# A two-way scan layer on one core: squares of the gated outputs move to GpSimd, their sums to transposes and VectorE, and all orders are new

## Chip, cores and metric

One core of a Trainium2 chip runs the whole kernel in one launch. The metric is device time in microseconds (us) from a run of the program; the profiled execution was recorded by the hardware profiler. Engines in the profile: PE is TensorE's matmul and PEld its weight load, DVE is VectorE, ACT is ScalarE, POOL is GpSimd, SP is SyncE.

## What is computed

Input x has 8 batches of 512 tokens with 256 channels. Each batch is normalised, goes through a selective-scan block in both token orders, is added back, normalised again, and goes through a linear layer with a low-rank correction.

```
zxbcdt = x @ Win                         # 256 -> 512 z, 512 x, 64 B, 64 C, 8 dt
xBC = silu(conv(xBC, convw, 4 taps) + convb)
dt = softplus(dt + dtb); dA = exp(dt * -exp(Alog))
h = dA_t * h + dt_t * outer(x_t, B_t)    # 8 heads of 64 x 64, token by token
y = C_t . h;  y = y + D * x
y = y * silu(z)
y = y * rsqrt(mean(y * y, over 512) + 1e-5) * normw
out = concat(y_fwd @ Wout_f, flip(y_rev @ Wout_b)) @ Wo + bo
```

All arithmetic is fp32; the projections run as three passes over split high and low parts.

## The kernel before, in words

Channels lie on the 128 partitions and tokens along the row, four chunks of 128. A scan works chunk by chunk in matrix form. `project` (L485 to L487) fills a PSUM bank with 128 channels of one direction, nine tiles in all: tile 0 holds B and C, tiles 1 to 4 the inputs x, tiles 5 to 8 the gates z. `conv_start` (ScalarE, L934) and three `conv` steps (VectorE, L1406) are the convolution, `conv_end` (L943) its Silu, and the ScalarE `gate` (L948) the Silu of z. `dt_project`, `dt_transposed` (L515) and the `soft_` steps give dt; `sums` and `s_transposed` (L530) give the running decays, which `row_copy` (L920) and `row_decays` (L925) write out so that SyncE can spread them over all partitions (`put_rows`, `repeat_heads`, `put_decays`, `repeat_decays`). `bound` (L964) and `decay` (L970) turn them into factors, `weights` (VectorE, L1433) multiplies them by the scores. `b_tokens` (TensorE L536, ScalarE L989) and `x_tokens` (L545, VectorE L1418) transpose B and x to have tokens on partitions. `state` (L565) makes the chunk states from xw (`decayed_x` on GpSimd, L1906, which needs `w_end` from `decay_w`, L952). `intra` (L578) and `inter` (L590) add up the outputs of a pair of heads; `inter` p needs `decayed_c` p (GpSimd, L1912). `outputs` (VectorE, L1455) adds D times x, and GpSimd's `gate` (L1929) multiplies by silu(z), giving yg.

The mean square of yg over its 512 channels: ScalarE squares the four tiles (`square`, L984; the first into sqsum, the others in turn into two buffers sq), GpSimd adds them to sqsum (`add_square`, L1937), and TensorE's `squares` (L598) multiplies each 128 x 128 chunk of sqsum by a column of ones, so that each token's sum stands in column c of the bank, and VectorE copies the four columns to ss (L1468). GpSimd's `mean_square` and `rms_root` follow. Beside that `mix` (L612) projects yg, and VectorE's `mix` (L1476) scales it with rms and adds it to the residual xres. `norm2_`, `feed` and `store` finish the batch. The reversed scan of the last batch has its own ending (`last_square`, `last_sums`, ...), with squares on ScalarE.

The work is laid out by hand: each engine has its own list of steps for the opening, the first scan, the reversed scan, the forward scan and the last scan. A loop turn runs the reversed scan of batch b, beside which the forward projections of batch b + 1 run, and then the forward scan of batch b + 1, with the reversed projections of b + 1 and the second norm and feed of batch b. There are seven such turns. Between engines there are only semaphores, and each engine runs its list strictly in order. The small PSUM results share two banks, taken in turn in the order of the lists START, LOOP and LAST, so a result waits until the one before the last is drained. VectorE and GpSimd also run `s_neg` (L1388), `s_rest` (wd, L1394) and `keep_x` (L1847).

Three wait rules hold the parts of the squares together:

```
act.wait_ge(yg_ready, KI * u + t + 1)            # square: its tile of yg
act.wait_ge(sqsum_ready, u)                      # square 1: the use before is summed
pool.wait_ge(sq_step, KI * u + t + 1)            # add_square: its square
```

## Time and profile before

| | |
|---|---|
| median of 3 runs | 636.88 us (635.69 to 637.5) |
| profiled execution, its own time | 635.01 us |
| its span, first to last instruction | 633.2 us |
| mean granted TensorE clock | 0.997 of full speed |
| instructions | 13301 |

How to read it: busy time is the time in which an engine has an instruction in hand; the span is cut into stretches where that helps. The chain is followed back from the last instruction, at each step to what released it. A group is all instructions of one line and shape. TensorE's matmuls are pipelined: the record of each is longer than its distance to the next, which is what the chain's pieces show.

### The profile page before, as it was taken

The numbers are of one execution on the slowest core, as the hardware profiler recorded it, in microseconds if no ns is written. First come the engines' busy times: TensorE is split into PE (matmuls) and PEld (weight loads), VectorE is DVE, ScalarE is ACT, GpSimd is POOL, SyncE is SP. The second block draws the span as 40 slices with busy tenths as digits, with TensorE's granted clock in tenths as the row PEclk, the third lists the DMA queues.
The fourth block names the chain that finished last, engine by engine and source line by source line (L and its number), as shares of the span: only waits on it lengthen the run. The fifth ranks groups of instructions, "written<-read, shape, count | busy, mean of one in ns | idle before, by whom it ended". The sixth has DMA issues, their size and how long they took to land.

```text
span 633.2 us, 13301 instructions
## 1 busy us (share of the span) xinstructions
PE 602.9 (95%) x3996; PEld 492.4 (78%) x3996; DVE 510.0 (81%) x1056; ACT 545.8 (86%) x1220; POOL 363.1 (57%) x367
## 2 busy tenths in 40 slices
PE   2998999999999999999999999999999999999995
PEld 1676788887888878887888878888788878888784
DVE  3779788986979689797888869798797978788663
ACT  4799998979997998979989799889989799897862
POOL 1026656666575664765556675656647665465933
PEclk9999999999999999999999999999999999999998
DMA  7552614245160632407132361505416071332600
GB/s 223 158 180 92 208 23 132 57 119 192 25 184 0 193 116 65 144 9 248 51 126 83 98 211 25 182 3 177 131 29 180 1 217 59 101 111 67 211 1 33
DMA packets 43544, 70.70 MB, mean 112 GB/s; under 512 B 8000, under 2 KB 30592, under 8 KB 43520
## 3 DMA queue, kind: packets, MB, share of 16 engines
q1 hardware_dynamic: 43520, 70.40, 36.5%
q8 instruction: 12, 0.20, 0.1%
q14 instruction: 12, 0.10, 0.1%
HBM read 59.37 MB, written 4.72 MB: 101 GB/s over the span
## 4 chain that ended last, share of the span: by engine, by line
PE 80%; ACT 9%; DVE 5%; issue 3%; POOL 2%; DMA 0%; SPq 0%; POOLq 0%; ACTq 0%; DVEq 0%
PE mi L612 17%; PE pj L485 9%; PE py L578 9%; PE pj L487 9%; PE pj L486 9%; PE py L590 6%; PE mi L565 4%; PE mi L678 3%; PE mi L545 2%; PE mi L598 2%; ACT bs L964 2%; ACT L952 1%; DVE xdt L1418 1%; POOL xw L1906 1%; PE mi L671 1%
## 5 line engine op out<-in xcount | busy, mean ns | idle before, releaser
L1406 DVE SCALAR_TENSOR_TENSOR xc<-pj,cw,xc 128x509 f32<-128x509 f32 (+2 forms) x240 | 173.9, 742 | 20.5 <-ACT xc L934 19.1
L964 ACT ACTIVATE bs<-bs,s_all 128x128 f32<-128x128 f32 x512 | 159.3, 392 | 0.0
L1929 POOL TENSOR_TENSOR yg<-yg,sz 128x512 f32<-128x512 f32 x60 | 76.6, 1287 | 87.3 <-DVE yg L1455 87.3
L485 PE MATMUL pj<-xnt_hi,w_hi 128*128 128x512 f32 x288 | 121.2, 421 | 3.8 <-DVE xnt_lo L1323 2.9
L487 PE MATMUL pj<-xnt_hi,w_lo 128*128 128x512 f32 x288 | 114.1, 396 | 0.0
L486 PE MATMUL pj<-xnt_lo,w_hi 128*128 128x512 f32 x288 | 113.9, 395 | 0.0
L612 PE MATMUL mi<-wc,yg 128*128 128x256 f32 x480 | 110.9, 384 | 0.0
L612 PEld LDWEIGHTS mi<-wc,yg 128*128 128x128 f32 x480 | 88.7, 190 | 14.0 <-issue 3.2
L1937 POOL TENSOR_TENSOR sqsum<-sqsum,sq 128x512 f32<-128x512 f32 x45 | 57.9, 1287 | 60.7 <-ACT sq L984 60.0
L1433 DVE TENSOR_TENSOR bs<-bs,gm 128x512 f32<-128x512 f32 x128 | 85.9, 676 | 6.7 <-ACT bs L970 6.3
L1906 POOL TENSOR_TENSOR xw<-xdt,w_end 128x512 f32<-128x512 f32 x48 | 49.7, 1044 | 48.7 <-DVE xdt L1418 37.5
L970 ACT ACTIVATE bs<-bs 128x512 f32<-128x512 f32 x128 | 77.1, 622 | 0.2
L1418 DVE TENSOR_TENSOR xdt<-mi,dt 128x512 f32<-128x512 f32 x64 | 43.2, 687 | 36.2 <-PE mi L545 35.9
L485 PEld LDWEIGHTS pj<-xnt_hi,w_hi 128*128 128x128 f32 x288 | 54.7, 190 | 18.3 <-DVE w_lo L1293 3.3
L578 PE MATMUL py<-bs,xdt 128*64 128x128 f32 x1024 | 67.4, 277 | 1.6 <-DVE yg L1455 1.6
L934 ACT ACTIVATE xc<-pj,cb,cw 128x512 f32<-128x512 f32 x80 | 61.3, 766 | 8.3 <-PE pj L487 7.8
L578 PEld LDWEIGHTS py<-bs,xdt 128*64 128x64 f32 x1024 | 56.1, 137 | 13.7 <-issue 6.6
L487 PEld LDWEIGHTS pj<-xnt_hi,w_lo 128*128 128x128 f32 x288 | 54.4, 189 | 12.7
L1912 POOL TENSOR_TENSOR es<-cc,es 128x384 f32<-128x384 f32 x64 | 63.7, 1007 | 0.6
L486 PEld LDWEIGHTS pj<-xnt_lo,w_hi 128*128 128x128 f32 x288 | 54.8, 190 | 9.9
L590 PE MATMUL py<-es,hst 128*128 128x128 f32 x384 | 55.5, 281 | 0.2 <-DVE hst L1447 0.2
L590 PEld LDWEIGHTS py<-es,hst 128*128 128x128 f32 x384 | 49.3, 192 | 4.3 <-issue 2.9
(151 smaller groups left out, 1040.3 us busy)
## 6 DMA issues: line engine op xcount, KB each, us to landing
bs<-rows_dram SPq DMA_DIRECT2D x64, 512.0 KB, 5.0
es<-rows_dram SPq DMA_DIRECT2D x128, 96.0 KB, 3.3
cc<-bcm SPq DMA_DIRECT2D x32, 128.0 KB, 3.1
xres<-in_x SPq DMA_DIRECT2D x8, 512.0 KB, 3.8
out<-ot SPq DMA_DIRECT2D x32, 128.0 KB, 3.7
xin<-in_x SPq DMA_DIRECT2D x7, 512.0 KB, 4.1
cz<-bcm SPq DMA_DIRECT2D x16, 128.0 KB, 3.4
rows_dram<-s_rows SPq DMA_DIRECT2D x128, 4.0 KB
```

Source lines behind the costliest of these rows:

```text
L485: pe.matmul(ps[:], hi(k), xnt_hi[:, k, :], start=(k == 0), stop=False)
L486: pe.matmul(ps[:], hi(k), xnt_lo[:, k, :], start=False, stop=False)
L487: mm = pe.matmul(ps[:], lo(k), xnt_hi[:, k, :], start=False, stop=(k == KD - 1))
L578: pe.matmul(py[bank][HP * half:HP * half + HP, Q * c:Q * c + Q], xdt[:, c, HP * h:HP * h + HP], bs[:, h, Q * c:Q * c + Q], start=(c == 0), ...
L590: mm = pe.matmul(py[bank][:, Q * c:Q * c + Q], hst[:, j, p, :], es[:, p, Q * c:Q * c + Q], start=False, stop=(j == NC - 2), skip_group_che ...
L612: mm = pe.matmul(ps[:, D * i:D * i + D], yg[:, d, t, Q * c:Q * c + Q], wc[:, d, t, :], start=(t == 0), stop=(t == KI - 1))
L964: i = nc.scalar.activation(bs[:, h, Q * c:Q * c + Q], bs[:, h, Q * c:Q * c + Q], ACT.Relu, bias=s_all[:, d, 0, c, h:h + 1], scale=-1.0)
L970: nc.scalar.activation(bs[:, h, :], bs[:, h, :], ACT.Exp, scale=-1.0).then_inc(decayed, 1)
L1406: i = dve.scalar_tensor_tensor(xc[:, t, to], pj[bank][:, of], cw[:, d, t, KW - 1 - s:KW - s], xc[:, t, to], ALU.mult, ALU.add)
L1433: dve.tensor_tensor(bs[:, h, :], bs[:, h, :], gm[:], ALU.mult).then_inc(m_ready, 1)
L1912: pool.tensor_tensor(es[:, p, LATER[d]], cc[:, d, LATER[d]], es[:, p, LATER[d]], ALU.mult).then_inc(c2_ready, 1)
L1929: pool.tensor_tensor(yg[:, d, p, :], yg[:, d, p, :], sz[:, d, p, :], ALU.mult).then_inc(yg_ready, 1)
```

## The change

The squares of yg are taken by GpSimd (a product of the tile with itself) instead of ScalarE. TensorE's `squares` transposes the four chunks of sqsum into a PSUM bank instead of multiplying them by ones, and VectorE's `squares` sums the bank over its 128 columns per chunk instead of copying four columns. `b_tokens` transposes only B's 64 lanes, into 64 columns per chunk, with a semaphore instruction ahead of it, and ScalarE copies the 256 columns that now lie side by side. All lists of steps of all engines, and with them the lists of PSUM banks, are in a new order. `last_square` stays on ScalarE. The diff below is cut: of the opening, the first and the last scan nothing is shown, of VectorE's lists only two places. Indentation is reduced.

In the parts left out: in the opening, `dt_project` goes before the first `project`; ScalarE has `split_high` 0 and 1 and `split_dt_high`, VectorE the matching `split_low` and `split_dt_low`, ahead of the first `norm_high` and `norm_low`; the constants are loaded after the first weights. In the forward scan VectorE keeps s_neg and s_rest at its end, ahead of the last `outputs`.

```diff
--- before.py
+++ after.py
@@ the lists of banks @@
-START = (["a0", "a1", "dtm", "dtt", "w0", "w1", "w2", "w3", "0S", "0ST", "w4", "w5", "w6", "w7", "w8"]
-+ ["0bt", "0x0", "0x1", "0x2", "0s0", "0x3", "1S", "1ST", "0s1", "0s2"])
+START = (["a0", "a1", "dtm", "dtt", "w0", "w1", "w2", "w3", "0S", "w4", "0ST", "w5", "w6", "w7", "w8"]
++ ["0x0", "0bt", "0x1", "1S", "0s0", "1ST", "0x2", "0x3", "0s1", "0s2"])
 LOOP = ["1bt", "1x0", "1x1", "1x2", "1x3", "a0", "a1", "1s0", "1s1", "dtm", "dtt", "0ss", "0o0", "1s2",
-"0o1", "0S", "0ST", "0bt", "0x0", "0x1", "0x2", "0s0", "0x3", "1ss", "0s1", "0s2", "1o0", "1o1",
+"0o1", "0S", "0ST", "0x0", "0bt", "0x1", "0x2", "0x3", "0s0", "1ss", "0s1", "0s2", "1o0", "1o1",
 "1S", "1ST", "t0", "t1", "f0", "f1", "t2", "t3", "f2", "f3"]
-LAST = ["1x0", "1x1", "1x2", "1bt", "1x3", "1s0", "0ss", "1s1", "0o0", "1s2", "0o1", "1o0", "1o1"]
+LAST = ["1x0", "1x1", "1bt", "1x2", "1x3", "1s0", "0ss", "1s1", "0o0", "0o1", "1s2", "1o0", "1o1"]
 assert len(LOOP) % 2 == 0
@@ SyncE @@
 def turn(it, more):
+    copy_c(it + 1, 0)
     if more:
         load_x("loop", it, it + 2)
-    copy_c(it + 1, 0)
     put_rows("loop", it, it + 1, 0)
     repeat_heads(it + 1, 0, 0)
+    repeat_heads(it + 1, 0, 1)
+    repeat_heads(it + 1, 0, 2)
     put_decays(it + 1, 0)
-    repeat_heads(it + 1, 0, 1)
     repeat_decays(it + 1, 0, 0)
-    repeat_heads(it + 1, 0, 2)
     repeat_decays(it + 1, 0, 1)
+    repeat_heads(it + 1, 0, 3)
     repeat_decays(it + 1, 0, 2)
-    repeat_heads(it + 1, 0, 3)
     repeat_decays(it + 1, 0, 3)
+    copy_c(it + 1, 1)
     put_rows("loop", it, it + 1, 1)
     store("loop", it, it, 0)
     load_residual(it + 1)
+    put_decays(it + 1, 1)
     repeat_heads(it + 1, 1, 0)
...
@@ TensorE, b_tokens @@
+    alone(pe)
     for c in range(NC):
-        mm = pe.transpose(ps[:, P * c:P * c + P], bcm[:, d, Q * c:Q * c + Q], ident)
+        mm = pe.transpose(ps[:, NS * c:NS * c + NS], bcm[0:NS, d, Q * c:Q * c + Q], ident[0:NS, 0:NS])
@@ TensorE, squares @@
     for c in range(NC):
-        mm = pe.matmul(ps[:, c:c + 1], sqsum[:, Q * c:Q * c + Q], ones[:, 0:1], start=True, stop=True)
+        mm = pe.transpose(ps[:, Q * c:Q * c + Q], sqsum[:, Q * c:Q * c + Q], ident)
@@ TensorE @@
 def reversed_scan(phase, it, b, nxt):
     more = phase == "loop"
+    project(b, 1, NT - 1)
     b_tokens(phase, it, b, 1)
     x_tokens(phase, it, b, 1, 0)
-    project(b, 1, NT - 1)
     x_tokens(phase, it, b, 1, 1)
     x_tokens(phase, it, b, 1, 2)
     x_tokens(phase, it, b, 1, 3)
     norm_transposed(phase, it, nxt)
     scores(phase, it, b, 1)
     state(phase, it, b, 1, 0)
+    state(phase, it, b, 1, 1)
     wait_xnt(phase, it)
-    state(phase, it, b, 1, 1)
     project(nxt, 0, 0)
     dt_project(phase, it)
     project(nxt, 0, 1)
     project(nxt, 0, 2)
     dt_transposed(phase, it)
+    intra(b, 1, 0)
     squares(phase, it, b, 0)
     mix(phase, it, b, 0, 0)
     mix(phase, it, b, 0, 1)
     state(phase, it, b, 1, 2)
-    intra(b, 1, 0)
     intra(b, 1, 1)
     mix(phase, it, b, 0, 2)
     mix(phase, it, b, 0, 3)
     inter(phase, it, b, 1, 0)
-    sums(phase, it, nxt, 0)
     inter(phase, it, b, 1, 1)
     project(nxt, 0, 3)
-    project(nxt, 0, 4)
+    sums(phase, it, nxt, 0)
     intra(b, 1, 2)
     s_transposed(phase, it, nxt, 0)
     inter(phase, it, b, 1, 2)
+    project(nxt, 0, 4)
     intra(b, 1, 3)
     inter(phase, it, b, 1, 3)
     project(nxt, 0, 5)
@@ TensorE @@
 def forward_scan(phase, it, b, last):
     more = phase == "loop"
     project(b, 0, NT - 1)
+    x_tokens(phase, it, b, 0, 0)
     b_tokens(phase, it, b, 0)
-    x_tokens(phase, it, b, 0, 0)
     scores(phase, it, b, 0)
     x_tokens(phase, it, b, 0, 1)
     x_tokens(phase, it, b, 0, 2)
     project(b, 1, 0)
+    x_tokens(phase, it, b, 0, 3)
     state(phase, it, b, 0, 0)
-    x_tokens(phase, it, b, 0, 3)
     project(b, 1, 1)
     project(b, 1, 2)
     squares(phase, it, last, 1)
...
     mix(phase, it, last, 1, 2)
     mix(phase, it, last, 1, 3)
     sums(phase, it, b, 1)
+    intra(b, 0, 1)
+    inter(phase, it, b, 0, 1)
     project(b, 1, 3)
     project(b, 1, 4)
-    intra(b, 0, 1)
     s_transposed(phase, it, b, 1)
-    inter(phase, it, b, 0, 1)
+    intra(b, 0, 2)
     norm2_transposed(phase, it, last, 0)
-    intra(b, 0, 2)
     inter(phase, it, b, 0, 2)
     norm2_transposed(phase, it, last, 1)
     feed(phase, it, 0)
...
     norm2_transposed(phase, it, last, 2)
     intra(b, 0, 3)
     norm2_transposed(phase, it, last, 3)
-    inter(phase, it, b, 0, 3)
     feed(phase, it, 2)
     feed(phase, it, 3)
+    inter(phase, it, b, 0, 3)
     project(b, 1, 5)
     project(b, 1, 6)
     project(b, 1, 7)
@@ ScalarE @@
 def b_tokens(phase, it, d):
     ps, free = misc(phase, it, f"{d}bt")
-    src = ps[:].rearrange("p (c n) -> p c n", c=NC)[:, :, 0:NS]
-    nc.scalar.activation(btok[:], src, ACT.Copy).then_inc(free, 1)
+    nc.scalar.activation(btok[:], ps[:, 0:NC * NS].rearrange("p (c n) -> p c n", c=NC), ACT.Copy).then_inc(free, 1)
@@ ScalarE @@
 def reversed_scan(phase, it, b, nxt):
     more = phase == "loop"
     b_tokens(phase, it, 1)
-    bound(b, 1, 0)
     gate(b, 1, NT - 1)
     decay_w(b, 1)
+    bound(b, 1, 0)
+    norm_high(phase, it, 0)
     decay_e(b, 1)
-    norm_high(phase, it, 0)
     norm_high(phase, it, 1)
     decay(b, 1, 0)
     bound(b, 1, 1)
     bound(b, 1, 2)
+    conv_start(nxt, 0, 0)
     bound(b, 1, 3)
-    square(phase, it, b, 0, 3)
-    conv_start(nxt, 0, 0)
     decay(b, 1, 1)
     dt_bias(phase, it)
     decay(b, 1, 2)
     conv_start(nxt, 0, 1)
+    bound(b, 1, 4)
     soft_exp(nxt)
-    bound(b, 1, 4)
     decay(b, 1, 3)
+    decay(b, 1, 4)
     bound(b, 1, 5)
-    decay(b, 1, 4)
+    conv_start(nxt, 0, 2)
     decay(b, 1, 5)
     soft_log(nxt)
-    conv_start(nxt, 0, 2)
+    conv_end(nxt, 0, 0)
     bound(b, 1, 6)
-    conv_end(nxt, 0, 0)
+    decay(b, 1, 6)
     bound(b, 1, 7)
-    decay(b, 1, 6)
     decay(b, 1, 7)
+    row_copy(phase, it, 0)
     conv_start(nxt, 0, 3)
-    square(phase, it, b, 1, 0)
+    conv_end(nxt, 0, 1)
     conv_start(nxt, 0, 4)
-    row_copy(phase, it, 0)
-    square(phase, it, b, 1, 1)
     row_decays(phase, it, 0)
-    conv_end(nxt, 0, 1)
     gate(nxt, 0, 5)
     conv_end(nxt, 0, 2)
     conv_end(nxt, 0, 3)
     gate(nxt, 0, 6)
+    gate(nxt, 0, 7)
     conv_end(nxt, 0, 4)
-    square(phase, it, b, 1, 2)
-    square(phase, it, b, 1, 3)
-    gate(nxt, 0, 7)
@@ ScalarE @@
 def forward_scan(phase, it, b):
     more = phase == "loop"
     ahead = not (isinstance(b, int) and b == NB - 1)
+    bound(b, 0, 0)
     b_tokens(phase, it, 0)
     gate(b, 0, NT - 1)
     decay_w(b, 0)
-    bound(b, 0, 0)
-    decay_e(b, 0)
     decay(b, 0, 0)
     bound(b, 0, 1)
     conv_start(b, 1, 0)
     decay(b, 0, 1)
+    bound(b, 0, 2)
     conv_start(b, 1, 1)
-    bound(b, 0, 2)
+    decay_e(b, 0)
     bound(b, 0, 3)
+    conv_start(b, 1, 2)
     decay(b, 0, 2)
+    decay(b, 0, 3)
     bound(b, 0, 4)
-    conv_start(b, 1, 2)
-    decay(b, 0, 3)
+    decay(b, 0, 4)
     bound(b, 0, 5)
-    decay(b, 0, 4)
     bound(b, 0, 6)
+    conv_end(b, 1, 0)
     bound(b, 0, 7)
     decay(b, 0, 5)
     decay(b, 0, 6)
-    square(phase, it, b, 0, 0)
-    decay(b, 0, 7)
     conv_start(b, 1, 3)
     norm2_scale(b - 1, 0)
+    norm2_scale(b - 1, 1)
+    row_copy(phase, it, 1)
+    decay(b, 0, 7)
     norm2(phase, it, 0)
-    row_copy(phase, it, 1)
-    norm2_scale(b - 1, 1)
+    norm2(phase, it, 1)
+    norm2_scale(b - 1, 2)
     row_decays(phase, it, 1)
-    norm2_scale(b - 1, 2)
-    norm2(phase, it, 1)
     norm2_scale(b - 1, 3)
-    conv_end(b, 1, 0)
     norm2(phase, it, 2)
     norm2(phase, it, 3)
     if ahead:
         norm1_scale(b + 1, 0)
         norm1_scale(b + 1, 1)
     conv_start(b, 1, 4)
+    conv_end(b, 1, 1)
+    conv_end(b, 1, 2)
+    gate(b, 1, 5)
     if ahead:
         norm1_scale(b + 1, 2)
-    conv_end(b, 1, 1)
-    conv_end(b, 1, 2)
+    conv_end(b, 1, 3)
+    gate(b, 1, 6)
     if ahead:
         norm1_scale(b + 1, 3)
-    square(phase, it, b, 0, 1)
-    square(phase, it, b, 0, 2)
-    gate(b, 1, 5)
-    conv_end(b, 1, 3)
     conv_end(b, 1, 4)
-    gate(b, 1, 6)
     gate(b, 1, 7)
@@ VectorE @@
 def squares(phase, it, d):
     ps, free = misc(phase, it, f"{d}ss")
-    dve.tensor_copy(ss[:, d, :], ps[:, 0:NC]).then_inc(free, 1)
+    dve.tensor_reduce(ss[:, d, :], ps[:].rearrange("p (c n) -> p c n", c=NC), mybir.AxisListType.X, ALU.add).then_inc(free, 1)
@@ VectorE, reversed_scan @@
     norm_low(phase, it, nxt, 0)
     norm_low(phase, it, nxt, 1)
     state(phase, it, b, 1, 0)
+    state(phase, it, b, 1, 1)
     scores(b, 1)
-    state(phase, it, b, 1, 1)
...
-    outputs(b, 1, 0)
+    s_copy(phase, it, 0)
+    s_neg(phase, it, 0)
+    weights(phase, it, b, 1, 6)
     outputs(b, 1, 1)
-    s_copy(phase, it, 0)
-    mix(phase, it, b, 0, 3)
-    weights(phase, it, b, 1, 6)
+    weights(phase, it, b, 1, 7)
     conv(nxt, 0, 3, 1)
-    weights(phase, it, b, 1, 7)
+    outputs(b, 1, 2)
+    s_rest(phase, it, 0)
@@ GpSimd @@
+def square(phase, it, b, d, t):
+    u = 2 * b + d
+    pool.wait_ge(yg_ready, KI * u + t + 1)
+    if t == 0 and phase == "loop":
+        bank, used = misc_use(phase, it, f"{1 - d}ss")
+        pool.wait_ge(mi_full[bank], used + 1)
+    if t == 1 and phase == "loop":
+        pool.wait_ge(sqsum_ready, u)
+    if t == 3:
+        pool.wait_ge(sq_added, (KI - 2) * u + 1)
+    to = sq[:, (t - 1) % 2, :] if t else sqsum[:]
+    pool.tensor_tensor(to, yg[:, d, t, :], yg[:, d, t, :], ALU.mult).then_inc(sq_step, 1)
@@ GpSimd, reversed_scan @@
     decayed_x(phase, it, b, 1, 0)
     decayed_x(phase, it, b, 1, 1)
     decayed_state(phase, it, b, 1, 1)
+    square(phase, it, b, 0, 3)
     add_square(b, 0, 3)
     decayed_state(phase, it, b, 1, 2)
+    decayed_c(b, 1, 0)
+    decayed_c(b, 1, 1)
     decayed_x(phase, it, b, 1, 2)
     mean_square(phase, it, 0)
-    decayed_c(b, 1, 0)
+    decayed_c(b, 1, 2)
     rms_root(b, 0)
-    decayed_c(b, 1, 1)
-    decayed_c(b, 1, 2)
+    gate(b, 1, 0)
+    square(phase, it, b, 1, 0)
     decayed_c(b, 1, 3)
-    gate(b, 1, 0)
     gate(b, 1, 1)
+    square(phase, it, b, 1, 1)
     add_square(b, 1, 1)
     gate(b, 1, 2)
+    square(phase, it, b, 1, 2)
     gate(b, 1, 3)
     add_square(b, 1, 2)
+    square(phase, it, b, 1, 3)
     add_square(b, 1, 3)
@@ GpSimd, forward_scan @@
     rms_root(last, 1)
     decayed_c(b, 0, 2)
     gate(b, 0, 0)
-    decayed_c(b, 0, 3)
+    square(phase, it, b, 0, 0)
     norm2_neg(last)
     norm2_var(last)
+    if ahead:
+        norm1_neg(b + 1)
+        norm1_var(b + 1)
     norm2_root(last)
     norm2_shift(last)
     result_bias(phase, it, last)
     if ahead:
-        norm1_neg(b + 1)
+        norm1_root(b + 1)
     gate(b, 0, 1)
+    square(phase, it, b, 0, 1)
     if ahead:
-        norm1_var(b + 1)
-        norm1_root(b + 1)
         norm1_shift(b + 1)
+    decayed_c(b, 0, 3)
     gate(b, 0, 2)
     add_square(b, 0, 1)
+    square(phase, it, b, 0, 2)
     keep_x(b)
     add_square(b, 0, 2)
     gate(b, 0, 3)
```

## Rows read from the trace of the kernel before

**Rows 1.** Page, part 1: busy us (share of the span) xinstructions.

```profile
PE 602.9 (95%) x3996; PEld 492.4 (78%) x3996; DVE 510.0 (81%) x1056; ACT 545.8 (86%) x1220; POOL 363.1 (57%) x367
```

**Rows 2.** Page, part 4: the chain that ended last, by engine.

```profile
PE 80%; ACT 9%; DVE 5%; issue 3%; POOL 2%; DMA 0%; SPq 0%; POOLq 0%; ACTq 0%; DVEq 0%
```

**Rows 3.** Busy time by stretch: stretch, us, each engine, granted clock, DMA share, GB/s.

```profile
40.00:107.84 67.84, 64.16 (x448) 51.39 (x447) 58.07 (x119) 64.63 (x147) 40.51 (x39) 1.00 0.40 125
182.24:256.64 74.40, 73.44 (x496) 60.34 (x495) 61.97 (x130) 66.72 (x150) 46.14 (x47) 1.00 0.37 110
256.64:331.30 74.66, 73.61 (x496) 60.31 (x495) 63.96 (x130) 66.74 (x151) 46.15 (x47) 1.00 0.34 110
```

**Rows 4.** The chain in one turn: start us, us, what.

```profile
...
230.45 0.36 PE mi L515 x4
230.81 0.98 PE mi L598 x8
...
255.28 0.45 PE mi L536 x4
...
263.52 0.79 PE mi L598 x8
```

**Rows 5.** Groups of TensorE: line, shapes, count, busy us, mean ns, idle.

```profile
L598 PE MATMUL mi<-cst,sqsum 128*128 128x1 f32 x120 | 15.0, 246 | 0.1
...
L536 PE MATMUL mi<-cst,bcm 128*128 128x128 f32 x64 | 9.6, 272 | 0.0
```

**Rows 6.** Groups of ScalarE, the same columns.

```profile
L943 ACT ACT_TABLE_LOAD x24 | 30.8, 1283 | 0.4
L984 ACT ACTIVATE sq<-yg 128x512 f32<-128x512 f32 x45 | 26.6, 625 | 0.2 <-POOL yg L1929 0.2
```

**Rows 7.** Groups of GpSimd, the same columns.

```profile
L1929 POOL TENSOR_TENSOR yg<-yg,sz 128x512 f32<-128x512 f32 x60 | 76.6, 1287 | 87.3 <-DVE yg L1455 87.3
...
L1937 POOL TENSOR_TENSOR sqsum<-sqsum,sq 128x512 f32<-128x512 f32 x45 | 57.9, 1287 | 60.7 <-ACT sq L984 60.0
L1906 POOL TENSOR_TENSOR xw<-xdt,w_end 128x512 f32<-128x512 f32 x48 | 49.7, 1044 | 48.7 <-DVE xdt L1418 37.5 <-ACT w_end L952 11.2
```

**Rows 8.** Timeline of VectorE: start us, us, instructions in order.

```profile
251.76 1.07 DVE L1313 BATCH_NORM_STATS2 st<-xin 128x6 f32<-128x256 f32 x3
```

**Rows 9.** Timelines of TensorE and of ScalarE in one turn; idle in brackets.

```profile
220.68 0.66 PE L545 MATMUL mi<-cst,xs 128*128 128x128 f32 x4 [0.35 <-DVE xdt L1418]
...
222.12 0.66 PE L469 MATMUL mi<-cst,xin 128*128 128x128 f32 x4 [0.19 <-DVE xdt L1418]
...
224.47 0.65 PE L565 MATMUL mi<-xw,btok 128*64 128x256 f32 x4 [0.22 <-issue]
...
259.50 0.65 PE L565 MATMUL mi<-xw,btok 128*64 128x256 f32 x4 [0.20 <-POOL xw L1906]
...
256.64 1.28 ACT L952 ACT_TABLE_LOAD   x1
```

**Rows 10.** Groups of VectorE, columns as in rows 5.

```profile
L1418 DVE TENSOR_TENSOR xdt<-mi,dt 128x512 f32<-128x512 f32 x64 | 43.2, 687 | 36.2 <-PE mi L545 35.9
...
L1328 DVE TENSOR_REDUCE v<-mi 128x64 f32<-128x128 f32 x8 | 2.3, 291 | 6.0 <-PE mi L515 6.0
...
L1468 DVE COPY ss<-mi 128x4 f32<-128x4 f32 x15 | 2.3, 154 | 2.6 <-PE mi L598 2.6
```

**Rows 11.** Timelines of VectorE and of GpSimd at 291 us.

```profile
290.97 2.44 DVE L1394 TENSOR_TENSOR wd<-s_all 128x32 f32<-128x32 f32 x1
...
290.96 2.40 POOL L1847 TENSOR_TENSOR xres<-xres,bo_sb 128x1024 f32<-128x1024 f32 x1
```

**Rows 12.** Timeline of ScalarE, between row_copy and w_end.

```profile
251.14 0.60 ACT L948 ACTIVATE sz<-pj 128x512 f32<-128x512 f32 x1 [1.03 <-PE pj L487]
```

**Rows 13.** Timeline of GpSimd, and the chain, late in a forward scan.

```profile
280.80 1.27 POOL L1929 TENSOR_TENSOR yg<-yg,sz 128x512 f32<-128x512 f32 x1
...
283.62 1.02 PE py L578 x16
```

More of the change, by code:

```diff
@@ new lines, in first_scan @@
+                s_copy(phase, it, 1)
+                conv(b, 1, 0, 2)
+                conv(b, 1, 0, 3)
+                weights(phase, it, b, 0, 0)
+                s_neg(phase, it, 1)
+                conv(b, 1, 1, 1)
+                state(phase, it, b, 0, 0)
+                s_rest(phase, it, 1)
+                conv(b, 1, 2, 1)
+                conv(b, 1, 1, 2)
+                x_tokens(phase, it, 0, 3)
+                conv(b, 1, 1, 3)
+                x_tokens(phase, it, 0, 2)
+                weights(phase, it, b, 0, 1)
```

422 lines of the change are left out of this document (196 added, 226 removed).

## The prediction

> **What bounds the kernel now.** I read the busy shares first, then the chain, then busy time by stretch, then the timelines where two engines meet. TensorE is busy 95% of the span, ScalarE 86%, VectorE 81%, GpSimd 57% [rows 1]; a busy matmul row may still hold a wait, so the shares alone settle nothing. The chain that ended last puts 80% of the span on TensorE, 9% on ScalarE, 5% on VectorE and 2% on GpSimd [rows 2]. The stretches say why. One turn of the loop (one batch, both scans) takes 74.40 us, with TensorE busy for 73.44; ScalarE works 66.72, VectorE 61.97, GpSimd 46.14 [rows 3]. There are seven turns of this kind, an opening and a first batch before them and a tail behind. The granted clock is 1.00 there (the upper level, 2.4 GHz), so the clock is not in play. Inside a turn, what TensorE does not have to do comes off the time, as long as no other engine takes its place.
>
> **The squares' sums on TensorE.** Each of 15 uses is now 4 matmuls of one column; the trace has 120 instructions, so two passes per matmul [rows 5]. The chain gives a use 0.98 us in the reversed scan and 0.79 in the forward one [rows 4], mean 0.887: nearly all of it loads sqsum as the stationary operand, twice. The change makes them transposes. Transposes of just this shape exist: B's tokens have 64 instructions for 16 uses, so one pass each [rows 5], and four of them take 0.45 us in the chain [rows 4]. So a use falls by 0.44 us, and 15 save **6.6 us**. Ends: nothing, should a short group pay a slow start; at most 0.98 - 0.45 = 0.53 each, 8.0 us.
>
> **B's tokens** (16 uses) stay 4 transposes, but of 64 lanes and with 64 columns of identity. No row has that. The nearest is dt's transpose with 32 lanes and 32 columns, which takes 0.36 us for four [rows 4]; so most of the time does not follow the columns. Ends: 0.45 (no gain) and 0.22 (columns alone count). I take 0.37, next to that row: 0.08 x 16 = **1.3 us**. The semaphore instruction put ahead of them only holds a wait; I cost it at nothing, since matmuls of a projection are still in flight while it passes. ScalarE's copy still reads 256 columns: no change.
>
> **ScalarE.** It loses 60 Squares (45 to sq, in the row, and 15 to sqsum) at 0.625 us, 37.5 us [rows 6]. That looks like relief for the engine at 86%, but the new order gives it back. A table load costs 1283 ns [rows 6], and a turn now has seven (ahead of decay_w twice, soft_log, conv_end 0 and 1 of the reversed scan, its late decays, conv_end 0 of the forward scan). I walked the new lists with the same three families (Exp, Ln, Silu; the rest runs under any). In the forward scan conv_end(b, 1, 0) now stands between bound 6 and decay 5: one more load for it and one for the way back to Exp. In the reversed scan row_decays stands behind conv_end(nxt, 0, 1), and a Silu gate follows: two more. 4 x 1.283 = 5.1 us come to a turn, 8 x 0.625 = 5.0 go. ScalarE's work stays at 66.8 of 74 us. What counts is where the loads stand (rival 1).
>
> **GpSimd** gets the 60 squares. Its product of two such tiles takes 1287 ns; one with the same tile twice is not in the trace. Ends: 1044 (the cheapest row over 512 columns) and 1287 [rows 7]; I take 1287, the same two-input form: 77 us in all, 10.3 in a turn, 46.14 becomes 56.4 of 74. As a sum it is covered: it now waits 87 us for VectorE's outputs and 60 for ScalarE's squares [rows 7], and the latter go. Where the reversed scan ends, it must do gate 3, add 2, square 3 and add 3 (5.2 us) after VectorE's last output, which ends as the norm's statistics begin, at 251.76 [rows 8]: done at 257.0. decayed_x then waits for w_end, behind the table load that starts at 256.64 and takes 1.28 [rows 9]: covered, by about 1 us.
>
> **VectorE.** The copy of 4 sums (154 ns) becomes a sum over 512 columns of PSUM. In the rows 128 columns take 291 ns, so (291 - 154)/124 = 1.1 ns for each column more, 0.154 + 508 x 0.0011 = 0.71 us; a product over 512 columns at 0.687 is the other end [rows 10]. I take 0.70: +0.55 x 15 = 8.2 us, 1.1 in a turn, on an engine with 12 us free. In the reversed scan mix 0 waits for it (and a root on GpSimd), but TensorE mixes for 3.6 us meanwhile: covered.
>
> **A lock between VectorE and GpSimd.** wd (32 columns) takes 2.44 us from 290.97, and ends with GpSimd's keep_x of 2.40 us from 290.96 [rows 11]. That turn lasts 74.66 us against 74.40 [rows 3]: a stall of 2.2 us costs 0.26. More GpSimd work makes more such meetings, in the reversed scan above all, where s_neg now follows s_copy while the gates run. If every turn had one, 7 x 0.26 = 1.8 us, less what is there now. I take +0.5.
> The Trainium skill, "SBUF — State Buffer", Who interferes with whom, states that VectorE and GpSimd share a port pair, that VectorE wants it with two SBUF inputs or in a two-port mode, and that the later one is blocked for the whole instruction. By that rule 60 more GpSimd instructions are 60 more chances to block; the trace agrees (2.44 us for wd), and shows how little of it reaches the end.
>
> **The orders.** TensorE's idle in a turn is 0.96 us, and four rows make it up: 0.35 and 0.19 in the run of x_tokens and norm transposes, 0.22 before state 1, 0.20 before the forward state 0 [rows 9]. The new order puts x_tokens 3 ahead of that state 0 (four transposes of work, while xw comes), and state 1 straight behind state 0 instead of behind the wait for xnt: 0.42 go. The run of x_tokens stays paced by xdt (0.687 us [rows 10] for four transposes) and loses the projection in its midst: its stalls stay. So 0.42 x 7 = **2.9 us**, between nothing and 0.96 x 7 = 6.7. Other moves (intra 1 before two projections, sums later) swap work whose inputs are there. load_x on SyncE's queue goes behind copy_c, which waits for conv_end; it is issued some 17 us later, and still lands before 251.76, when the norm reads it. copy_c of the other direction goes ahead of put_rows, and its input comes earlier too: nothing. In the opening dt_project goes first and two splits stand ahead of it; I take that as even.
>
> **Sum**, against the profiled execution (635.01 us, 1.8 above its span): -6.6 - 1.3 - 2.9 + 0.5 = -10.3, so 624.7. The median of the runs, 636.88, is 1.87 above that execution; so **626.6 us**.
>
> **Rivals.**
> 1. *ScalarE's loads take the pace* (slower). From row_copy to the next scan's w_end the list gains two loads (2.57 us) and bound 0 (1.17) and loses four squares (some 0.52 each between neighbours): +1.6. w_end releases xw and so state 0. For it: the wait before state 0 is put down to xw [rows 9]. Against: ScalarE idles 1.03 us in that stretch for a projection [rows 12], which takes most of it up. From a surplus over 1 us on it decides; with all of TensorE's gain hidden and 0.6 more in each turn it is 636.9 + 7 x 0.6 = 641. Chance 0.11.
> 2. *GpSimd makes es late* (no change). In the forward scan decayed_c 3 now stands behind gate 1 and square 1. Gate 1 starts at 280.80 and takes 1.27 [rows 13]; a root goes ahead of it (1.0), square 1 (1.29), a shift and decayed_c itself (1.0) follow: 285.6. inter 3, moved behind two feeds (1.73), wants it 1.73 - 0.44 after intra 3 ends at 284.64 [rows 13], at 285.9. If the sequence is 1.5 us longer, TensorE stalls 1.2 in a turn: 7 x 1.2 = 8.4, so 635.0 to 635.5. For it: a margin of 0.3. Chance 0.10.
> 3. *The new transposes save TensorE little*, because each short group pays its start: 6.6 becomes nothing, 633.2. Against it: 0.45 for four of them in the chain. Chance 0.12.
> 4. *More stalls go than I count*: the other 0.54 us of idle in a turn too (3.8), and 2 of the 3.7 us by which TensorE misses the stretch from 40 to 107.84 [rows 3]: 621. Chance 0.17.
>
> **Numbers.** My case has 0.50. Faster by over 0.3% (what a measurement of this kernel can tell from no change, 1.9 us) are my case, 3 and 4: 0.79; within it 2: 0.10; slower 1: 0.11. Range: from 619, a little under case 4, to 637, past case 2; case 1 is left out, and little else.
>
> **What would show it.** The sums' transposes at x60, four in 0.45 us; B's in 0.37; turns of about 73 us with TensorE idle for 0.5; no Square but the four at the end; 28 more table loads and ScalarE still near 546 us; GpSimd near 440. I am wrong if turns stay at 74 with TensorE idle before state 0 (rival 1) or inter 3 (rival 2), or if a group of these transposes takes 0.8.

## The result, and the profile after

The changed kernel takes 638.4 us (median; 637.7 to 639.17, 14 runs) against 636.81 for the kernel before on the same chip (635.69 to 637.5, 14 runs): ratio 1.0029, 95% interval 1.0021 to 1.0037. It is slower by 1.6 us by the medians and 1.8 by the ratio, just under the bound of 0.3% for a difference; I had forecast 626.6, in a range up to 637.

Page of the changed kernel: busy time and share of each engine, and the chain that ended last; it answers to [rows 1, 2].

```profile
span 637.0 us, 13185 instructions
PE 606.5 (95%) x3936; PEld 482.2 (76%) x3936; DVE 524.6 (82%) x1056; ACT 552.2 (87%) x1188; POOL 422.7 (66%) x427
PE 75%; ACT 11%; DVE 9%; issue 3%; POOL 1%; DMA 0%; SPq 0%; ACTq 0%; DVEq 0%; POOLq 0%
```

TensorE lost 60 matmuls, as meant, but only its weight loads are less busy (482 us against 492); its matmuls are busy for 606.5 us against 602.9. ScalarE has 60 Squares less and is 6 us busier (28 more table loads, as walked); GpSimd rose from 57% to 66%. The chain has less TensorE in it and more ScalarE and VectorE.

One turn of it by stretch, the columns of [rows 3], and the groups that are new (busy us, mean ns, idle before and its releaser):

```profile
148.05:222.67 74.62, 73.78 (x487) 58.81 (x487) 64.47 (x130) 67.96 (x147) 54.13 (x55) 1.00 0.37 112
L599 PE MATMUL mi<-cst,sqsum 128*128 128x128 f32 x60 | 9.4, 279 | 0.0
L1442 DVE TENSOR_REDUCE ss<-mi 128x4 f32<-128x512 f32 x15 | 10.3, 685 | 4.0 <-PE mi L599 4.0
L1916 POOL TENSOR_TENSOR sq<-yg 128x512 f32<-128x512 f32 x45 | 46.9, 1041 | 1.8
```

A turn still takes 74.6 us, where I had said 73. The prices of single instructions came out near what I took, or below: the sum over columns 0.685 us (taken 0.70), GpSimd's square 1.04 (taken 1.29: with the same tile on both sides it is at the cheap end). Four transposes of sqsum are dearer: 0.49 and 0.53 from their start to the next group's (taken 0.45).

Where the 3.8 us between the two profiled spans lie (single executions; the medians are 1.6 us apart). Turns here run from the first norm transpose of one turn to that of the next. From the start of the loop's first turn to that of the seventh (six turns) the kernel before takes 519.50 - 72.31 = 447.19 us, the changed one 521.22 - 73.41 = 447.81: 74.53 and 74.64 a turn. The stretch before the first turn is 1.1 longer; 0.4 of that is a later change of TensorE's pace, no work of the change (last section). The other 0.7 is there again between x1 and x7 (first turn at 73.27 and 73.17) and x4 and x6 (73.94 and 73.90), which open like the changed kernel; I had taken the opening as even. In the seventh turn both reach the last scan's x tokens after 69.8 us; from there on, 43.9 us are left before (589.35 to 633.2) and 45.9 after (591.05 to 637.0). Part of that may belong to the execution: x7 and x14 below have the same code there and take 43.6 and 45.0. In the changed kernel TensorE idles there ahead of the tokens, for nothing that the profile shows, and behind VectorE:

```profile
592.86 0.43 PE L537 MATMUL mi<-cst,bcm 64*128 64x64 f32 x4 [0.75 <-issue]
598.88 5.42 PE L613 MATMUL mi<-wc,yg 128*128 128x256 f32 x24 [0.29 <-DVE ss L1442]
```

The puzzle is in the turns: by my count TensorE was given 0.9 us less work for the sums in each, and a turn did not get shorter.

### The profile page after: what moved, and what is told of

Read it like the earlier page. It is cut to its first block, busy times and chain, and to the rows that moved or that the text cites. A ratio compares the mean times of both kernels' runs of the same rounds, so it can differ in the third digit from the quotient of the medians.

```text
span 637.0 us, 13185 instructions
## 1 busy us (share of the span) xinstructions
PE 606.5 (95%) x3936; PEld 482.2 (76%) x3936; DVE 524.6 (82%) x1056; ACT 552.2 (87%) x1188; POOL 422.7 (66%) x427
## 4 chain that ended last, share of the span: by engine, by line
PE 75%; ACT 11%; DVE 9%; issue 3%; POOL 1%; DMA 0%; SPq 0%; ACTq 0%; DVEq 0%; POOLq 0%
PE mi L613 16%; PE py L579 8%; PE pj L485 8%; PE pj L487 7%; PE pj L486 7%; PE py L591 5%; PE mi L679 4%; PE mi L566 4%; PE mi L546 4%; DVE xc L1380 2%; ACT xs L944 2%; PE gm L553 2%; ACT sz L949 2%; DVE xdt L1392 2%; ACT xc L935 2%
## 5 line engine op out<-in xcount | busy, mean ns | idle before, releaser
L487 PE MATMUL pj<-xnt_hi,w_lo 128*128 128x512 f32 x288 | 114.0, 396 | 0.0
L579 PE MATMUL py<-bs,xdt 128*64 128x128 f32 x1024 | 69.2, 277 | 1.2 <-DVE bs L1407 0.7
L487 PEld LDWEIGHTS pj<-xnt_hi,w_lo 128*128 128x128 f32 x288 | 54.3, 189 | 12.8
L1894 POOL TENSOR_TENSOR hs<-hst,e_end 128x512 f32<-128x512 f32 x32 | 33.4, 1044 | 36.5 <-ACT e_end L956 19.0
L591 PE MATMUL py<-es,hst 128*128 128x128 f32 x384 | 53.9, 280 | 0.3 <-DVE hst L1421 0.2
```

What stands on the lines that cost most here:

```text
L487: mm = pe.matmul(ps[:], lo(k), xnt_hi[:, k, :], start=False, stop=(k == KD - 1))
L579: pe.matmul(py[bank][HP * half:HP * half + HP, Q * c:Q * c + Q], xdt[:, c, HP * h:HP * h + HP], bs[:, h, Q * c:Q * c + Q], start=(c == 0), ...
L591: mm = pe.matmul(py[bank][:, Q * c:Q * c + Q], hst[:, j, p, :], es[:, p, Q * c:Q * c + Q], start=False, stop=(j == NC - 2), skip_group_che ...
```

## The experiments

Each run has the kernel before beside it on the same chip; ratios are to that. "Turn" is the mean of turns 1 to 6, read as above.

```
run                                     ratio   95% interval      turn us
changed kernel                          1.0029  1.0021 to 1.0037  74.64
x1  sums by transposes only             1.0005  0.9995 to 1.0015  74.55
x2  squares on GpSimd only              1.0068  1.0053 to 1.0084  74.88
x3  all three operations, old orders    1.0109  1.0093 to 1.0126  75.36
x4  new orders, sums by ones            1.0063  1.0048 to 1.0079  74.92
x5  small squares (work left out)       1.0077  1.0063 to 1.0091  75.05
x6  small sum (work left out)           0.9969  0.9958 to 0.9979  74.15
x7  x1, sum covered                     0.9921  0.9908 to 0.9934  73.80
x8  new orders, three moves             1.0151  1.0136 to 1.0166  75.55
x9  x7 and B's tokens                   0.9941  0.9928 to 0.9954  73.91
x10 new orders, cover only              1.0044  1.0031 to 1.0058  74.65
x11 x9 and squares on GpSimd            1.0092  1.0077 to 1.0106  75.20
x12 x9, states together                 0.9944  0.9930 to 0.9958  73.91
x13 x7, GpSimd squares behind xw        1.0219  1.0204 to 1.0233  76.25
x14 x7, states together                 0.9931  0.9917 to 0.9944  73.82
```

### Operations or orders?

My first theory was that the operations pay and the new orders give it back. x1 to x3 put operations alone into the kernel before; x4 takes one out of the changed kernel.

```
x1  mm = pe.transpose(ps[:, Q*c:Q*c+Q], sqsum[...], ident)   # for pe.matmul(.., ones[:, 0:1])
    dve.tensor_reduce(ss[:, d, :], ps[...], X, ALU.add)      # for dve.tensor_copy(ss, ps[:, 0:NC])
x2  square(...) out of the lists of act; into those of pool: 0, 1 behind gates 0, 1; 2, 3 ahead of gate 3 and add 3
x3  x1 + x2 + B's tokens from 64 lanes
x4  changed kernel, L599 and L1442 as in the kernel before
```

> The kernel before with its own orders; only the squares' sums go by four transposes and VectorE's sum over columns. Theory (the operations pay, the new orders give it back): the reversed use keeps its 0.35 us per turn, the forward use loses it to the wait of state 2 for the bank that VectorE's sum holds, so 634.3 us, 2.5 below the kernel before (between 632.5 and 635.5). Rival (the transposes save TensorE nothing that counts, since other engines set the pace): 636.4 to 637.4. Rival (my forecast's own term, no bank wait): 630.8.

> The kernel before with its own orders; only the squares of gated outputs move from ScalarE to GpSimd, each in GpSimd's list behind its gate or ahead of its addition. Theory: ScalarE's 60 squares were covered, GpSimd has the room, some VectorE instructions are held beside GpSimd's: 637 us, within 0.7 of the kernel before. Rival (GpSimd's load and the lock are what the change pays): slower by 2 us or more, 639 and above. Rival (ScalarE sets the pace in places): faster by 2 us or more, 635 and below.

> The kernel before with its own orders and all three changed operations (GpSimd's squares, sums by transposes, B's tokens from 64 lanes). Theory (the operations pay and the new orders give it back): the sum of the first two and about 0.5 for B's tokens, 633.5 us (632 to 635), so 5 below the changed kernel. Rival (operations give nothing, orders neutral): 636.5 to 638.5.

> The changed kernel with its new orders, the squares' sums back to the matmul with the column of ones and the short copy. Theory: it loses the reversed use's gain and gets back the bank wait, so 639.9 us, 1.0 to 2.5 slower than the changed kernel. My forecast's term: 6.6 slower, 645. Rival (transposes save nothing): within 0.5 of the changed kernel's 638.4.

The theory fell. x1 gains nothing, x2 costs 0.7% and x3 1.1%: in the old orders the operations themselves lose 7 us, and the new orders win 5 of them back (x3 against the changed kernel). Only x4 came as expected: in the new orders the transposes give 0.28 us a turn, a third of what I had counted.

The waits of TensorE in x1 (us in total, times, longest) say what took its saving:

```profile
PE mi L523 <- DVE al L1376: 3.4, 8, 1.0
PE mi L565 <- DVE ss L1468: 1.6, 7, 0.4
```

In the kernel before, the first of these is one wait of 1.0, and the second isn't there; the wait for xw is 1.4 in both. What is new comes from VectorE's sum. Forward, it still holds its PSUM bank when state 2, two uses on, wants it. Reversed, it stands in VectorE's list between the steps of the softplus (du, rq, dd ... al), so that al comes 20.5 us into the turn instead of 20.0 and is late for the decays' sums. VectorE and TensorE of x1 there:

```profile
233.86 0.68 DVE L1468 TENSOR_REDUCE ss<-mi 128x4 f32<-128x512 f32 x1
242.84 0.18 DVE L1376 TENSOR_SCALAR al<-adt 128x32 f32<-128x32 f32 x1
243.08 0.41 PE L523 MATMUL mi<-al,cst 128*128 128x32 f32 x2 [0.38 <-DVE al L1376]
```

### Is VectorE's sum the price, and what does GpSimd's load cost in the new orders?

```
x5  pool.tensor_tensor(to[:, 0:32], yg[.., 0:32], yg[.., 0:32], mult)      # changed kernel, from the loop on
x6  dve.tensor_reduce(ss, ps[...][:, :, 0:8], X, ALU.add)                  # changed kernel
x7  x1, forward:  state 1, intra 0, state 2      # for state 1, state 2, intra 0
        reversed: inter 0, inter 1, sums         # for inter 0, sums, inter 1
x8  changed kernel, forward as in x7; project(b, 1, NT-1) between x tokens 0 and 1; row_decays ahead of conv_end 1
```

> The changed kernel; from the loop on, each of GpSimd's squares covers 32 of the 512 columns (the first scan's stay whole), so some 57 squares of 1.04 us shrink to a fraction and the output leaves out most of the squares. Turns of the changed kernel are 74.6 us. Theory A (in the new orders GpSimd's squares are off the path, ScalarE's xs and w_end pace the reversed end): turn 74.4 to 74.6, time 637 to 638.4. Theory B (GpSimd's load still costs in the new orders, through xw, es or the lock on VectorE): turn 74.3 or less, time 636.5 or below, 2 us or more under the changed kernel.

> The changed kernel; VectorE's sum goes over 8 of each 128 columns, so 0.69 us shrinks to some 0.1 to 0.2 and the output leaves out most of the sum. Theory (the bank that the sum holds delays state 2 in the forward half, 0.2 us of idle and a restart per turn; the reversed sum is covered): turn 0.3 less, 74.3, time 636.0 to 636.8. If the sum costs in both halves: turn 0.6 less, time 634. If nowhere: 638.4.

> The kernel before with its own orders and ScalarE's squares, sums by transposes (as in the first run), and two moves on TensorE: forward, the first intra is put ahead of state 2, so that VectorE's sum is over when state 2 wants the bank; reversed, the sums of the decays go behind the second inter. Theory (the transposes save 0.35 to 0.44 per use, and what took it back were VectorE's sum ahead of the decay chain and the bank): the waits for ss (1.6) and for al (3.4) fall to about 1 in all, turn 74.0, time 4 below the kernel before, 632 to 633. Rival (the saving is lost to something else, with or without the waits): turn 74.4 to 74.6, time within 1 us of the kernel before.

> The changed kernel with three moves back or ahead: forward, the first intra ahead of state 2 (cover for VectorE's sum); reversed, the last projection of the direction back between x tokens 0 and 1; ScalarE's row decays ahead of the convolution's end 1 (two table loads less). Theory (each of the three is one of the places where the new orders gave the gain back, 0.2 to 0.25 us per turn each): turn 74.0 to 74.2, time 634.5 to 635.5. Rival (the orders are balanced, a move only shifts the wait): turn 74.5 to 74.8, time 638 to 639.5.

**x7** settles the sums. Two moves on TensorE, and 0.75 us a turn appear against x1; the time is 0.79%, 5.0 us, below the kernel before. Turn and rows of x7:

```profile
147.04:220.81 73.77, 72.77 (x487) 59.24 (x487) 63.05 (x129) 66.60 (x151) 46.18 (x47) 1.00 0.36 111
240.32 1.50 PE L590 MATMUL py<-es,hst 128*128 128x128 f32 x12
241.66 0.31 PE L523 MATMUL mi<-al,cst 128*128 128x32 f32 x2
263.14 0.65 PE L565 MATMUL mi<-xw,btok 128*64 128x256 f32 x4
263.62 1.04 PE L578 MATMUL py<-bs,xdt 128*64 128x128 f32 x16
264.49 0.60 PE L565 MATMUL mi<-xw,btok 128*64 128x256 f32 x4
```

All twelve matmuls of the two inters run through, and the decays' sums no longer wait; the intra of 16 matmuls covers the bank. The two idles that went showed 0.38 and 0.20 us; the turn fell by 0.75 (in six turns TensorE's idle fell by 3.1 us and its busy time by 1.4), so a wait costs more than the idle that the trace shows. x6, below, has the same: 0.20 of idle, 0.38 of turn. What is left fits the uses: 0.98 and 0.79 us before [rows 4], 0.55 and 0.53 in x7 (230.26 to 230.81, 262.61 to 263.14), 0.69 a turn against 0.73 measured between the kernel before and x7.

**x6** agrees from the other side: with a short sum in the changed kernel the turn falls by 0.49. In its turn from 148.03, state 1 and state 2 run as one group of eight, and 0.38 of the 0.49 lie between there and the mix.

**x8** was worse than either theory had it. TensorE's waits in its turn (0.68 us for ScalarE's xs, 0.40 for xnt_lo before state 0, 0.47 before a mix for state 2) stand at two of the moves: with the projection behind them, x tokens 0 come one projection too early for xs; and the mix meets VectorE's state 2 (x10 shows that one alone). The third move took two table loads a turn from ScalarE and no wait in the trace answers to it. Here, and in x10, the moves only shifted waits.

**x5** is the surprise: with 44 us less work on GpSimd (378 us busy instead of 423) the kernel got slower, by 0.4 us a turn. VectorE, GpSimd and TensorE of x5:

```profile
250.10 1.26 DVE L1368 TENSOR_TENSOR wd<-s_all 128x32 f32<-128x32 f32 x1
248.35 1.30 POOL L1902 TENSOR_TENSOR yg<-yg,sz 128x512 f32<-128x512 f32 x1
250.04 1.27 POOL L1925 TENSOR_TENSOR sqsum<-sqsum,sq 128x512 f32<-128x512 f32 x1
253.39 0.50 PE L485 MATMUL pj<-xnt_hi,w_hi 128*128 128x512 f32 x1 [0.49 <-DVE xc L1380]
```

and the same wd in the changed kernel, where GpSimd's addition starts at 250.44 and wd is past:

```profile
249.05 0.24 DVE L1368 TENSOR_TENSOR wd<-s_all 128x32 f32<-128x32 f32 x1
```

The short square lets the addition start 0.06 us ahead of wd; wd, of 32 columns, then lasts as long as the addition, the convolutions behind it slip by 1 us, and a projection waits 0.49 for its bank, in each turn. So x5 can't price GpSimd's load; what it shows is that a shift of GpSimd's addition (26.3 us into the turn instead of 27.8, with wd at 26.3 and 26.4) makes a lock on VectorE or none.

### The parts on top of the covered sums

```
x9   x7 + B's tokens from 64 lanes
x10  changed kernel, forward: intra 0 ahead of state 2
x11  x9 + squares on GpSimd, placed as in x2
x12  x9 + reversed: state 0, state 1, then the wait for xnt
```

> The run with covered sums (own orders of the kernel before, two moves on TensorE), and B's tokens from 64 lanes added. Theory: a use of the tokens' transposes falls from 0.44 to 0.39 us from start to the next start, 15 uses, 0.7 us: about 0.1 per cent below the run with covered sums, 631.1 against a kernel before of 636.8. Rival (ScalarE's copy or the wait ahead of the transposes eats it): equal to the run with covered sums or slower by up to 1 us.

> The changed kernel, in the forward half the first intra ahead of state 2 and nothing else. Theory (the bank that VectorE's sum holds is all that is wrong at this place): the wait for ss goes, turn 74.3 to 74.4, time 636.5. Rival (in the new orders VectorE's state 2 comes so that the mix then waits for it, as the run with three moves hinted with 0.5 us per turn): turn 74.8 to 75.0, time 640.

> The run with covered sums and B's tokens, and the squares moved to GpSimd, each behind its gate or ahead of its addition. Theory (GpSimd's squares and additions push xw at the turn of direction, whatever the sums cost): turn 0.35 to 0.8 longer than without them, the time 4 to 6 us above the run with covered sums and B's tokens. Rival (the earlier price was made by the sums' own waits): within 1.5 us of it.

> The run with covered sums and B's tokens, and the reversed half's states 0 and 1 put together ahead of the wait for the normed input, as in the new orders. Theory: the changed kernel's gain at this place, 0.2 us per turn, 7 turns: 1.3 us below the run with covered sums and B's tokens, about 629.8 against a kernel before of 636.8. Rival (GpSimd's xw 1 or the bank makes state 1 wait): equal or slower.

**x9** is 0.2% slower than x7, where I had a gain. The 95% intervals overlap a little, but all its turns are longer, by 0.11 us on average, and x12 against x14 below, where B's tokens are the only difference too, repeats it (73.91 against 73.82 us a turn, ratios 0.13% apart). TensorE around B's tokens in x7:

```profile
254.08 0.40 PE L487 MATMUL pj<-xnt_hi,w_lo 128*128 128x512 f32 x1
254.32 0.60 PE L536 MATMUL mi<-cst,bcm 128*128 128x128 f32 x4
254.75 0.60 PE L545 MATMUL mi<-cst,xs 128*128 128x128 f32 x4
255.19 1.06 PE L552 MATMUL gm<-cz,bcm 128*128 128x128 f32 x8
```

and in x9:

```profile
254.53 0.40 PE L487 MATMUL pj<-xnt_hi,w_lo 128*128 128x512 f32 x1
254.86 0.46 PE L537 MATMUL mi<-cst,bcm 64*128 64x64 f32 x4
255.25 0.66 PE L546 MATMUL mi<-cst,xs 128*128 128x128 f32 x4
255.75 1.06 PE L553 MATMUL gm<-cz,bcm 128*128 128x128 f32 x8
```

The transposes themselves fall from 0.43 to 0.39 us. But the projection ahead takes 0.33 instead of 0.24 to hand over, and the full-size transposes behind them 0.50 instead of 0.44: from L487 to gm 1.22 us against 1.11. A use costs 0.1 more in both halves, 0.2 a turn, and about half of it reaches the turn. The rest of the 0.2% lies behind the last scan's x tokens, where x9 takes 44.8 us and x7 43.6; x14, without this change, takes 45.0, so that part is not the tokens'. Whether the 64-lane shape or the semaphore instruction ahead of it does that stays open; without the instruction it wasn't tried.

**x11** prices GpSimd's squares: 1.5%, 9.7 us, 1.29 a turn. Its turn from reversed to forward:

```profile
255.24 1.31 POOL L1903 TENSOR_TENSOR yg<-yg,sz 128x512 f32<-128x512 f32 x1 [1.53 <-DVE yg L1429]
256.62 1.04 POOL L1917 TENSOR_TENSOR sq<-yg 128x512 f32<-128x512 f32 x1
257.62 1.27 POOL L1903 TENSOR_TENSOR yg<-yg,sz 128x512 f32<-128x512 f32 x1
258.86 1.28 POOL L1925 TENSOR_TENSOR sqsum<-sqsum,sq 128x512 f32<-128x512 f32 x1
260.08 1.05 POOL L1917 TENSOR_TENSOR sq<-yg 128x512 f32<-128x512 f32 x1
261.29 1.29 POOL L1925 TENSOR_TENSOR sqsum<-sqsum,sq 128x512 f32<-128x512 f32 x1 [0.16 <-POOL sq L1917]
262.53 1.05 POOL L1880 TENSOR_TENSOR xw<-xdt,w_end 128x512 f32<-128x512 f32 x1
263.72 0.65 PE L566 MATMUL mi<-xw,btok 128*64 128x256 f32 x4 [1.45 <-POOL xw L1880]
```

Between the gate's release by VectorE's output and xw there is no room left: six instructions in a row, then xw, then TensorE, which has idled 1.45 us. In six turns TensorE's idle goes from 5.6 us (x9) to 13.4, its busy time stays at 437.8 (437.9): the wait for xw is the whole price of a turn. In x7 the same place has four (two gates, two additions), and GpSimd idles 1.09 us for w_end before xw:

```profile
257.57 1.05 POOL L1906 TENSOR_TENSOR xw<-xdt,w_end 128x512 f32<-128x512 f32 x1 [1.09 <-ACT w_end L952]
```

xw starts 36.8 us into the turn in x7 and x9 and 38.1 in x11; the turns differ by 1.4 and 1.3. Of the delay 0.3 is VectorE's, whose outputs start 30.0 us into the turn instead of 29.7 (neg_s lasts 0.51 there), and the rest is GpSimd's queue. In the same way x2 (wait up to 0.6 us) and x3 (up to 0.9) lie between: I read this as one effect (argued from these runs, not shown apart): the longer VectorE's list makes the outputs late, the longer GpSimd's queue makes xw late, and the less TensorE has to do, the more of it shows.

**x10** confirmed its rival in the mechanism: the wait for ss went, and a mix waited 0.5 us for state 2 on VectorE, 7 times, 3.3 us in all; the turn did not move (74.65). **x12** won 0.2 us at the states and lost it on the way: the decays' sums start 20.86 us into the turn in x9 and 20.71 in x12, the projections behind the next inters at 27.84 and 27.81. That VectorE's chain holds them is argued from the first of these, not shown.

### Queue place or load?

```
x13  x7 + squares on GpSimd; xw 0 of the forward scan ahead of add 2, square 3, add 3
x14  x7 + reversed: state 0, state 1, then the wait for xnt
```

> The run with covered sums (B's tokens as in the kernel before), squares on GpSimd, and at the turn from reversed to forward GpSimd's xw 0 goes ahead of the last two additions and the last square. Theory (the price is the place in the queue): TensorE's wait for xw falls from 1.5 us a turn to 0.3 or less, turn 73.9 to 74.2 against 73.8 with ScalarE's squares, ratio to the kernel before 0.993 to 0.996. Rival (the load itself costs, since the queue is full from the gates to the states and the wait only moves on to xw 1, xw 2 or the state's product): turn 74.6 or more, ratio 1.001 or more.

> The run with covered sums, and the reversed half's states 0 and 1 together ahead of the wait for the normed input; B's tokens as in the kernel before. Theory (the 0.2 us saved per turn is used up by the wait for VectorE's decay chain behind the second inter): turn 73.75 to 73.8, ratio within 0.1 per cent of the run with covered sums, 0.9921. Rival: the gain shows, turn 73.6, ratio 0.990.

x13's rival holds in its number: the kernel is 2.2% slower than before and 3.0% slower than x7, twice the price in x11. xw 0 now comes in time, and the wait moves on to xw 1 and xw 2 (1.13 and 0.55 us) and to the sums:

```profile
265.36 0.65 PE L565 MATMUL mi<-xw,btok 128*64 128x256 f32 x4 [0.20 <-POOL xw L1880]
270.94 0.65 PE L565 MATMUL mi<-xw,btok 128*64 128x256 f32 x4 [1.13 <-POOL xw L1880]
273.02 0.65 PE L565 MATMUL mi<-xw,btok 128*64 128x256 f32 x4 [0.55 <-POOL xw L1880]
282.02 0.38 PE L523 MATMUL mi<-al,cst 128*128 128x32 f32 x2 [0.58 <-DVE xres L1450]
```

But GpSimd is not full here. With xw 0 ahead of the last additions it first stands idle for ScalarE's w_end, and everything else comes behind that:

```profile
264.18 1.04 POOL L1880 TENSOR_TENSOR xw<-xdt,w_end 128x512 f32<-128x512 f32 x1 [2.30 <-ACT w_end L952]
```

xw 0 starts 36.7 us into the turn (38.1 in x11), but the es behind it 41.4 (39.1). So moving the one instruction is no remedy; whether the load costs wherever the squares stand is not shown, since a place that uses these 2.30 us wasn't tried. x14 confirms that the states put together bring nothing: the turn is x7's.

### What the new orders do to TensorE

Six turns of the kernel before, of x11 and of the changed kernel, columns of [rows 3]:

```profile
72.31:519.50 447.19, 441.11 (x2966) 362.03 (x2965) 375.55 (x774) 401.01 (x901) 276.89 (x277) 1.00 0.36 109
74.10:525.28 451.18, 437.78 (x2917) 353.23 (x2917) 385.68 (x774) 378.15 (x853) 325.57 (x325) 1.00 0.35 107
73.41:521.22 447.81, 442.66 (x2917) 352.81 (x2917) 386.81 (x775) 407.84 (x877) 325.30 (x326) 1.00 0.37 109
```

x11 and the changed kernel have the same operations and the same count of matmuls. The new orders take 1.4 us a turn off TensorE's idle time (13.4 us to 5.2 in six turns; the wait for xw goes) and add 0.8 to its busy time (437.78 to 442.66). Taken from one start to the next, waits over 0.15 us left out, the x tokens now take 4.36 us a turn instead of 3.76, intra 8.22 instead of 7.84, the feeds 3.55 instead of 3.27; inter and mix give back 0.4 and 0.3. The x tokens of the reversed scan can be followed. In the old orders a projection stands behind the first group, and the four groups take 2.34 us without it (x7: 217.00 to 217.36, 218.83 to 220.81). In the new orders they stand together and take 2.89, 0.72 each, next to VectorE's xdt of 0.69:

```profile
219.78 1.20 PE L546 MATMUL mi<-cst,xs 128*128 128x128 f32 x8
221.22 1.25 PE L546 MATMUL mi<-cst,xs 128*128 128x128 f32 x8 [0.24 <-DVE xdt L1392]
```

No run moves these parts one by one, so which moves cost what is read from the traces, not shown by experiment.

## Why the prediction was wrong

My terms made a turn 74.53 - 0.88 (sums) - 0.16 (B's tokens) - 0.42 (idles) + 0.07 (lock) = 73.1 us; it takes 74.6. Of the 1.5 us missed, 0.6 is the sums' missing cover (x4: they give 0.28), 0.3 is B's tokens (x9: +0.11, measured in the old orders), and 0.6 the orders and GpSimd's squares together.

**Step "VectorE": "covered".** The failing step of the largest term. The saving on TensorE is there, a little smaller than I had it (a use takes 0.54 in x7, not 0.45, so 0.35 are saved, 5.2 us in 15 uses where I had 6.6), and x7 shows all of it: 5.0 us. But I costed the sum of 0.70 us by VectorE's free time in a turn and looked only at mix 0 behind it. Two others wait for VectorE there: the bank (state 2, forward) and al (the decays' sums, reversed). Without the two moves of x7 the gain is nil (x1). The new orders cover the reversed one and not the forward one ([<-DVE ss] seven times, 1.5 us), so the changed kernel keeps 0.28 us a turn (x4), and a short sum would give it 0.49 more (x6).

**Step "GpSimd": "as a sum it is covered".** In the changed kernel the stretch that I walked comes out nearly so: add 3 ends 36.4 us into the turn (257.0 is 35.7 into its own), and xw waits for w_end, 0.80 us where I had about 1:

```profile
259.83 3.04 POOL L1879 TENSOR_TENSOR xw<-xdt,w_end 128x512 f32<-128x512 f32 x3 [0.80 <-ACT w_end L953]
```

That holds only in the new orders, where VectorE's output 2 goes 4.5 us ahead of output 3 (248.39 and 252.86), so that gate 2 and square 2 are past. In the old ones the two outputs follow each other directly, six instructions stand behind them instead of the four that I counted, and x11 measures 9.7 us. So the squares bring no gain of their own and are covered only by the new orders, whose price on TensorE I had at nothing. What the squares cost in the new orders isn't shown alone: x5 was to tell it and met a lock instead.

**Step "ScalarE".** The 28 loads are as walked. The 60 squares had been worth only 27 us of busy time (x2: 545.8 to 518.4), not 37.5, so ScalarE ends at 552 and not near 546. That the relief buys nothing was right: no wait of TensorE in the turns of the kernel before is put down to ScalarE. The rival on ScalarE has no run behind it: xw waits for w_end and starts 37.2 us into the turn instead of 36.8 to 37.1, yet TensorE's wait before the forward state 0 is gone, since x tokens 3 stand ahead of it.

**Step "B's tokens": 1.3 us saved.** Wrong in sign: 0.11 us a turn lost (x9 against x7; 0.09 in x12 against x14), some 0.8 us in all. I priced the group alone; the loss is in its neighbours.

**Step "the orders": 2.9 us saved.** I had the other moves as an even swap of "work whose inputs are there", and the x tokens' run as one that only keeps its stalls when it loses the projection in its midst. The two idles that I let go did go, but a turn's idle fell only from 1.01 to 0.86 us, as the wait for ss came in, and the moves that I had at nothing cost TensorE 0.8 us of busy time a turn (changed kernel against x11). The projection had been cover for VectorE's xdt. Against x3 the new orders save 0.72 us a turn, 5 us, because there they also make room for GpSimd's squares; against x9, which leaves the squares on ScalarE, the changed kernel is 0.73 us a turn longer, of which x6 puts 0.49 on VectorE's sum.

**The rivals.** None came true as written. Rival 1 had the right sign from the wrong engine. Rival 2 (es late) did not occur: decayed_c 3 ended at 286.76 and inter 3 came at 287.65; counted from the turn's start (1.4 us later than in the kernel before) that is 0.2 earlier and 0.35 later than I had walked, a margin of 0.9 us instead of 0.3. Rival 3 (transposes save little) is what x1 looks like, from another cause.

The account by runs, each step a difference of ratios: sums with cover -0.79% (x7), B's tokens +0.20% (x9), squares on GpSimd +1.51% (x11), new orders -0.63% (changed kernel against x11); together +0.29%, what was measured (they add up by construction). The step for B's tokens is as large as its interval, and the last one also holds the cover of x7 that the new orders drop.

x7 beats both kernels: 631.19 us, ratio 0.9921 to the kernel before.
